# Causal cross-attention: exponents straight from PSUM, head by head, in place of VectorE's subtraction

## What is computed

```python
qp = q @ Wq.T                                  # q: layer-normed x, 16 x 128 x 256
kv = latent_kv @ Wkv_expand.T                  # latent_kv: 16 x 128 x 64
k, v = jnp.split(kv, 2, axis=-1)               # 16 heads of 16
scores = jnp.einsum('bhqd,bhkd->bhqk', qh, kh) * inv_sqrt_d      # inv_sqrt_d = 16 ** -0.5
causal = jnp.tril(jnp.ones((sq, sk), dtype=bool))
scores = jnp.where(causal, scores, jnp.finfo(scores.dtype).min)
attn = jax.nn.softmax(scores, axis=-1)
out = jnp.einsum('bhqk,bhkd->bhqd', attn, vh)
return out @ Wout.T                            # added to x
```

## Time and profile before

| what | value |
| --- | --- |
| median of 3 runs | 1540.8 us (1540.37 to 1540.9) |
| the profiled execution's own time | 1528.9 us |
| its span, first to last instruction | 1526.9 us |
| TensorE's mean granted clock | 0.924 of full speed |
| the cross stage in the span | about 1175 to 1374 us |

### The profile page before, as it was taken

How to read it: one execution, slowest core, us unless ns; L and a number is a source line. 1 busy time by engine, 2 the same in 40 slices (tenths; PEclk the granted TensorE clock), 3 DMA queues, 4 the chain that set the end, 5 groups by cost and what they waited for, 6 DMA issues and landing times. The chain is left out here.

```text
span 1526.9 us, 26276 instructions
## 1 busy us (share of the span) xinstructions
PE 1270.9 (83%) x7886; PEld 995.6 (65%) x7886; DVE 1009.6 (66%) x1953; ACT 831.0 (54%) x1870; POOL 644.0 (42%) x724
## 2 busy tenths in 40 slices
PE   6994888885794998648989998999887898988998
PEld 5672555554683897536777777777775555657887
DVE  5997888884353444797777777777774566643443
ACT  5452888883352455556666666666654465552332
POOL 2003555554336015467666666666664323310000
PEclk9996999997797999969999999999999899998999
DMA  8401333310003454020000000000000000000000
GB/s 306 151 0 30 95 82 82 82 42 1 1 25 119 136 188 142 28 100 0 2 1 0 0 0 0 0 0 0 0 1 3 5 3 3 3 0 1 15 14 28
DMA packets 49684, 64.52 MB, mean 42 GB/s; under 512 B 6032, under 2 KB 42896, under 8 KB 48336
## 3 DMA queue, kind: packets, MB, share of 16 engines
q1 hardware_dynamic: 46544, 55.27, 11.5%
q0 software_dynamic: 3072, 8.39, 1.6%
HBM read 38.48 MB, written 16.78 MB: 36 GB/s over the span
## 5 line engine op out<-in xcount | busy, mean ns | idle before, releaser
L2180 ACT ACTIVATE wi_weights<-wi_psum,wi_bias,wi_scale 128x128 f32<-128x128 f32 x256 | 113.7, 453 | 114.5 <-DVE wi_bias L2290 114.5
L1955 POOL TENSOR_TENSOR wi_straight<-wi_straight,wi_crossed 128x512 f32<-128x512 f32 x80 | 109.7, 1371 | 5.8 <-DVE wi_crossed L2276 5.8
L959 DVE TENSOR_REDUCE gq_top<-gq_psum 128x4 f32<-128x512 f32 x128 | 86.6, 677 | 28.7 <-PE gq_psum L846 28.0
L1943 POOL TENSOR_TENSOR wi_scratch<-wi_sums,wi_eps 128x4 f32<-128x4 f32 x80 | 36.1, 451 | 158.5 <-DVE wi_sums L2259 157.2
L913 ACT ACTIVATE gq_weights<-gq_weights 128x512 f32<-128x512 f32 x128 | 81.1, 634 | 22.0 <-DVE gq_weights L967 20.6
L2281 DVE TENSOR_REDUCE wi_top<-wi_psum 128x4 f32<-128x512 f32 x64 | 44.0, 687 | 73.7 <-PE wi_psum L2070 73.7
L853 PE MATMUL gq_psum<-const,gq_weights 128*128 128x128 f32 x512 | 79.4, 279 | 14.9 <-ACT gq_weights_t L919 14.9
L1944 POOL TENSOR_TENSOR wi_scale<-wi_scratch,minus_half 128x4 f32<-128x4 f32 x80 | 84.6, 1058 | 6.3
L967 DVE TENSOR_TENSOR gq_weights<-gq_psum,gq_top 128x512 f32<-128x512 f32 x128 | 87.0, 680 | 0.0
L919 ACT ACTIVATE gq_weights_t<-gq_psum 128x512 f32<-128x512 f32 x128 | 75.9, 594 | 12.0 <-PE gq_psum L853 11.3
L2092 PE MATMUL wi_psum<-wi_wo_high,wi_out_high 128*128 128x256 f32 x256 | 47.2, 308 | 41.7 <-DVE wi_out_low L2244 39.0
(11 more groups left out here) (383 smaller groups left out, 3924.2 us busy)
## 6 DMA issues: line engine op xcount, KB each, us to landing
gq_keys<-in_ctx_keys_dram SPq DMA_DIRECT2D x16, 512.0 KB, 3.9
gq_keys_diagonal<-gq_key_parts SPq DMA_DIRECT2D x64, 128.0 KB, 3.9
slot_x<-rw_zero SPq DMA_DIRECT2D x1, 5120.0 KB, 17.9
ex_slot_rows<-slot_x SPq DMA_DIRECT2D x20, 256.0 KB, 2.9
slot_y<-ex_s_out SPq DMA_DIRECT2D x20, 256.0 KB, 2.1
x<-in_x_dram SPq DMA_DIRECT2D x4, 512.0 KB, 8.6
gate<-in_gate_dram SPq DMA_DIRECT2D x2, 1024.0 KB, 5.6
up<-in_up_dram SPq DMA_DIRECT2D x2, 1024.0 KB, 7.9
```

The costliest lines, as they stand in the source:

```text
L959: dve.tensor_reduce(top[:, u % 4, :], rows(u), AX.X, ALU.max).then_inc(topped, 1)
L1955: added_up = pool.tensor_tensor(straight[:, at], straight[:, at], crossed[:, at], ALU.add)
L2180: act.activation(weights[:, g % 2, j, :], ps[:, SC + g % 2, j * P:j * P + P], ACT.Exp, bias=bias[:, g % 2, j:j + 1], scale=scale[:, g, j:j ...
```

## The change

The exponents read the masked scores in PSUM, and the subtraction goes into the exponent's bias. ScalarE computes exp(scale x input + bias) with one bias for each partition, and a row has another extreme for each head, so each head needs an instruction of its own: four of 128x128 in place of one of 128x512.

For the bias to be the extreme itself and not its negative, scores and mask are negated: the constant that spreads the keys is -1 in place of 1 and the mask is +1e30 in place of -1e30. VectorE takes the minimum, and the exponent has scale -1. The factor 16 ** -0.5 moves into the row scale of the layer norm (variance and epsilon times 16). The wait for the weights' buffer moves from VectorE to ScalarE, and a bank is free for the next mask when its exponents are done.

```diff
-def layer_norm_scale(pool, own, net, scratch, aggregated, ready, head):
+def layer_norm_scale(pool, own, net, scratch, aggregated, ready, head, widen=1.0):
...
-    inverse_root(pool, own, net.rstd[:, of], net.mean_var[:, of, 1], scratch[:, of], 1.0, LN_EPS,
+    inverse_root(pool, own, net.rstd[:, of], net.mean_var[:, of, 1], scratch[:, of], widen, widen * LN_EPS,
...
-    SCALE = float(XHD) ** -0.5
+    WIDEN = float(XHD)
...
-        top, out_t = sb("cr_top", [P, 2, 4]), sb("cr_out_t", [P, BANK])
+        least, out_t = sb("cr_least", [P, U, 4]), sb("cr_out_t", [P, BANK])
...
-                    need(pe, shifted, U * (t - 1) + u + 1)
+                    need(pe, weighed, U * (t - 1) + u + 1)
...
             def weigh(t, s, u):
-                act.wait_ge(shifted, U * t + u + 1)
-                act.activation(weights[:, s, u], weights[:, s, u], ACT.Exp, scale=SCALE).then_inc(weighed, 1)
+                act.wait_ge(bounded, U * t + u + 1)
+                if begun(t, 2):
+                    act.wait_ge(turned, number("p", t - 2, u) + 1)
+                for j in range(4):
+                    e = act.activation(weights[:, s, u, j * P:j * P + P], ps[:, u, j * P:j * P + P], ACT.Exp,
+                                       bias=least[:, u, j:j + 1], scale=-1.0)
+                e.then_inc(weighed, 1)
...
-            def shift(t, s, u):
+            def bound(t, u):
 
                 dve.wait_ge(scored, U * t + u + 1)
-                rows = ps[:, u, :].rearrange("p (j t) -> p j t", t=P)
-                link(dve.tensor_reduce(top[:, u % 2, :], rows, AX.X, ALU.max))
-                if begun(t, 2):
-                    dve.wait_ge(turned, number("p", t - 2, u) + 1)
-                dve.tensor_tensor(weights[:, s, u].rearrange("p (j t) -> p j t", t=P), rows,
-                                  wide(top[:, u % 2, :], [P, 4, P]), ALU.subtract).then_inc(shifted, 1)
+                dve.tensor_reduce(least[:, u, :], ps[:, u, :].rearrange("p (j t) -> p j t", t=P), AX.X,
+                                  ALU.min).then_inc(bounded, 1)
...
-    const[:, CONST["causal"]] = np.where(distance >= 0, 0.0, FAR)
+    const[:, CONST["causal"]] = np.where(distance >= 0, 0.0, -FAR)
...
-    const[:, CONST["half"]] = (p[:, None] // XHD) % 2 == np.arange(2)[None, :]
+    const[:, CONST["half"]] = -((p[:, None] // XHD) % 2 == np.arange(2)[None, :]).astype(np.float32)
```

More of the change, by code:

```diff
@@ L201, in inverse_root, with scale_of @@
     return pool.tensor_tensor(out, scratch, half, ALU.pow)
-def scale_of(pool, own, net, scratch, aggregated, ready, first, end):
+def scale_of(pool, own, net, scratch, aggregated, ready, first, end, widen=1.0):
     of = slice(first, end)
     pool.wait_ge(aggregated, end)
-    inverse_root(pool, own, net.rstd[:, of], net.mean_var[:, of, 1], scratch[:, of], 1.0, LN_EPS,
+    inverse_root(pool, own, net.rstd[:, of], net.mean_var[:, of, 1], scratch[:, of], widen, widen * LN_EPS,
                  net.half[:, of]).then_inc(ready, 1)
-def layer_norm_scale(pool, own, net, scratch, aggregated, ready, head):
+def layer_norm_scale(pool, own, net, scratch, aggregated, ready, head, widen=1.0):
     for first, end in ((0, head), (head, NB)):
-        scale_of(pool, own, net, scratch, aggregated, ready, first, end)
+        scale_of(pool, own, net, scratch, aggregated, ready, first, end, widen)
 def rwkv(nc, net, sem):
@@ L2425, in cross @@
         scored = sem("cr_scored")
-        shifted = sem("cr_shifted")
+        bounded = sem("cr_bounded")
         weighed = sem("cr_weighed")
@@ L2449, in _ @@
             own = Own(pool, own_pool)
-            layer_norm_scale(pool, own, net, scratch, aggregated, rstd_ready, 1)
+            layer_norm_scale(pool, own, net, scratch, aggregated, rstd_ready, 1, WIDEN)
             pool.memset(values[:], 0.0).then_inc(values_set, 1)
@@ L2731, in one @@
                 for u in range(U):
-                    shift(t, s, u)
+                    bound(t, u)
                     if u == 1 and begun(t, 2):
```

## The result

| | before | after |
| --- | --- | --- |
| median of 5 runs | 1540.9 us | 1548.31 us |
| lowest to highest | 1540.37 to 1542.58 | 1546.03 to 1548.7 |
| ratio | | 1.0044, 95% interval 1.0031 to 1.0058 |
| the profiled execution | 1528.9 us | 1548.7 us |

The change costs 7.4 us, between 4.8 and 8.9 by the interval. 1547.7 was forecast.

The account below looks back on a forecast made before the run. The prediction took a loop through TensorE, ScalarE's queue and GpSimd to set the 11.23 us tile. 6.3 - 0.4 + 1.0 = +6.9 us on 1540.8 gave 1547.7 us, range 1542.0 to 1555.0.

Parts of the forecast that it names:

- The pitch: On ScalarE, start-to-start time of one 128x128 exponent read from PSUM with a bias column, taken as 0.26 us.
- D: Time added to ScalarE's queue per head group: four exponents take 1.04 us where one took 0.52, so 0.52 us.
- Both routes: Two estimates for one small exponent on ScalarE: from windowed exponents 0.255 us, from PSUM copies with one column 0.25 us.
- The steady tile: In tiles 1 to 14 the `cr_qk` copy comes 0.45 us later per tile, +6.3 us in all.
- the two slacks: In a steady tile: 0.19 us between `cr_h_t` copy and query projection, 0.59 us on ScalarE ahead of the `cr_qk` copy.
- First tiles: In the first tile VectorE sets the pace and exponents start sooner, -0.4 us; the next counts as steady, +0.45 us.
- Last tile: Exponents 1 and 2 stand right ahead of the `cr_out_t` copy TensorE waits for, so both delays count: +1.0 us.
- The sum: Over the changed stage, steady tiles 6.3, first tile -0.4 and last tile +1.0 make +6.9 us.
- Dearer pieces: Rival: small exponents on ScalarE 0.29 to 0.36 us apart, costing +11 to +22 us, 1552 to 1563 us; chance 0.13.
- nothing to measure: Rival: small exponents on ScalarE near 0.20 us apart, costing +1 us, 1541.8 us; chance 0.12.
- The clock falls: Rival: added waits drop TensorE to half clock for projection, mask and scores in every tile, 1572 us; chance 0.04.
- The clock, the other way: Rival: TensorE's full clock returns sooner in three places, 7.6 us in all against +6.9, giving 1540.1 us; chance 0.06.

Follow-up runs that it names:

- e5: Kernel before with each 128x512 exponent cut into four of 128x128, in place in SBUF with a zero bias column, subtraction kept; 1553.52 us, ratio 1.0081.
- e1: Changed kernel with the exponents of u=1 moved behind the cr_h_t copy and those of u=2 behind the cr_qk copy; 1539.91 us, ratio 0.9991.
- e3: Changed kernel with only the exponents of u=2 moved behind the cr_qk copy; 1544.60 us, ratio 1.0025.
- e4: Changed kernel with one 128x512 exponent per head group, using the first head's extreme as bias for all four heads; 1538.83 us, ratio 0.9983.
- e6: Changed kernel with an unused 128x512 subtraction on VectorE behind each minimum; 1550.13 us, ratio 1.0059.
- e2: Changed kernel with only the exponents of u=1 moved behind the cr_h_t copy; 1558.45 us, ratio 1.0111.
- e8: Changed kernel with the exponents of u=1 and u=2 moved later and the keys projected earlier; 1540.15 us, ratio 0.9993.

## Why the prediction was right

- **The pitch.** Forecast 0.26 us a piece, D = 0.52. Measured 1.01 and 1.00 for four, 0.25 a piece, D = 0.48 to 0.49. Both routes in the prediction, 0.255 and 0.25, were closer than the value chosen. The Trainium skill's figure (ScalarE: Activation LUTs, What ACT_TABLE_LOAD costs) gave 0.294 and 1552.0: too dear for reads of PSUM by 0.04, and right out of SBUF, 0.29 in e5.
- **The steady tile.** Forecast +0.45, measured +0.44 by the `cr_qk` copies, at the place named: e1, e3 and e5 each give the growth that the two slacks say. By its own numbers D = 0.485 makes only 0.38, and from weights copy 3 to the `cr_qk` copy the growth is that, 2.88 to 3.24 us on the mean of the tiles. The missing 0.06 is the handover, a term that the prediction had at nothing: GpSimd starts 0.86 us behind the `cr_qk` copy's start instead of 0.77, since that copy lasts 0.68 us instead of 0.60. In before the row is

```profile
1238.90 1.23 POOL L2459 TENSOR_TENSOR cr_keys_diagonal<-cr_qk,const 128x256 f32<-128x256 f32 x2 [7.41 <-ACT cr_qk L2631]
```

- **First tiles.** Forecast -0.4 for tile 0 and +0.45 for the next. Measured -1.27 (10.54 instead of 11.81) and +0.85 (12.62 instead of 11.77). In tile 0 the `cr_h_t` copy came 0.55 us sooner and the query projection 0.49, as argued (0.50). The rest is the clock: that projection took 1.29 us where the earlier trace rows has 2.08, so nothing was given back but 0.79 gained.

```profile
1203.40 0.44 ACT L2623 ACTIVATE cr_h_t<-cr_psum 128x256 f32<-128x256 f32 x1
...
1203.89 1.29 PE L2501 MATMUL cr_psum<-cr_h_t,xwq 128*128 128x128 f32 x8 [1.92 <-ACT cr_h_t L2623]
```

  In the next tile, where mask and scores run at about half clock in both kernels, it stayed low longer: the scores took 2.09 us for 1.92, the first turns 1.38 for 1.10, and the first weights copy started 0.46 later.
- **Last tile.** Forecast +1.0. TensorE's wait for `cr_out_t` grew from 1.10 to 2.14 us, that 1.0. Only 0.4 remained at the stage's end, since its last projection was at full clock, 1.13 us instead of 1.83. First the two rows of after, then that of before:

```profile
1380.21 0.66 PE L2554 MATMUL cr_psum<-const,cr_out_t 128*128 128x128 f32 x4 [2.14 <-ACT cr_out_t L2655]
...
1391.69 1.13 PE L2570 MATMUL cr_psum<-xwout,cr_out_f 128*128 128x256 f32 x4 [0.47 <-ACT cr_out_f L2659]
```

```profile
1371.83 1.83 PE L2570 MATMUL cr_psum<-xwout,cr_out_f 128*128 128x256 f32 x4 [0.47 <-ACT cr_out_f L2654]
```

- **The sum.** In the traces tile 0 gives -1.3 (forecast -0.4), the fourteen tiles behind it +6.2 (+6.3), the end of the stage +0.4 (+1.0), the next stage, where the clock stayed low a little longer, +0.6 (nothing): +6.0, beside 7.4 by the medians and 6.9 forecast. Ahead of the first `cr_qk` copy TensorE also waited 0.49 us for a DMA instead of 0.23, which is not in that sum. The loop, which is nearly all of it, came as argued. That the sum of the small terms, -0.3 by the traces and +0.6 forecast, lies no farther off is partly luck: the clock took 0.8 and 0.7 us off two of them and added 0.6 to the third, none of which was forecast.
- **VectorE.** Worth nothing in steady tiles (e4, e6), as read from the waits. Its busy time on the page fell from 1009.6 to 967.0 us, 42.6 where 44.2 were announced.
- **Where it was off.** The pieces last 0.36 to 0.49 us each, with a median of 0.40, not 0.35 to 0.37; only their pitch matters to the queue. The profiled execution was forecast at 1535.8 and took 1548.7. The difference to the median was carried over as if it belonged to every profile; it was the expert stage of one execution.
- **The rivals.** "Dearer pieces" falls with the measured pitch and "nothing to measure" with the ratio. "The clock falls" did not happen: the clock is 1.00 in the steady tiles with waits of 0.25, 0.37 and 0.65 us. In e5, with 0.36, 0.49 and 0.65, it stayed too; in e2, with 0.91 and 0.65, it fell in four tiles and stayed in the others. I gave it 4 in 100 by TensorE's share over the tile; how near the change came to it no run shows. "The clock, the other way" came in two small pieces, 0.8 us in tile 0 and 0.7 in the last, and other places gave about 1 us back.

## What to carry to other kernels

Before cutting one instruction into several, find its place in the queue of the engine that runs it, and what copies stand behind it. Taking work from an engine that nobody waits for gains nothing. Giving work to one that has 40% idle time costs whatever exceeds the slack at that place of its queue: here 0.97 us of added work ahead of the `cr_qk` copy met 0.59 us of slack. The cheapest experiment is to change the order and keep the work: it gave all of the loss back here, and the list of waits then showed a larger gain of another kind.

## What the runs showed of the hardware that was not expected

- TensorE's clock fell to about half for mask and scores in four tiles of e2 (0.87 over the tile), with no wait of TensorE over 0.91 us in the trace's list for this stretch. The tiles around them have the same waits of 0.91 and 0.63 to 0.66 us at full clock, so the waits allow it but don't settle it. With 0.65 us of filler in the first wait all steady tiles stayed at full clock. With 0.49 and 0.65 us (e5) and with 0.36 and 0.30 us (e8) they stayed too.
- The copies of 128x512 out of PSUM got longer behind the exponents that read PSUM with a bias column, though their own work is the same. Behind two groups of four, 0.67 us (`cr_out_t`) and 0.68 (`cr_qk`) in after, where before has 0.60, and GpSimd starts 0.09 us later. Behind one group, 0.62 and 0.60 in e1; behind pieces out of SBUF, 0.58 in e5. Why is not shown.
